# Score banks in a ring of five and a single y bank, in an attention kernel with two fused layers

## The reference

```
x = x + 0.5 * ffn(layernorm(x))
x = x + attn(layernorm(x))
x = x + 0.5 * ffn(layernorm(x))

ffn(x)  = x @ W.T + b + (x @ V_r) @ C.T          # 256 -> 256, rank 32 correction
attn(x): 16 heads of 16; causal; no softmax:
    att = polymax(q @ k.T / sqrt(16))
    y   = att @ v;   return y @ W_proj
polymax(s) = (s**2 + 1) / 1000        for s > 0
             (1 - s / 100) / 1000     for -100 <= s <= 0
             0                        below -100, and where masked
```

## Time and profile before

| | |
|---|---|
| median of 3 runs | 2130.39 us (2128.72 to 2139.16) |
| the profiled execution | 2134.19 us, span 2132.5 us |
| TensorE (PE) busy | 1797.4 us, 84% |
| VectorE (DVE) busy | 1707.9 us, 80% |
| ScalarE (ACT) busy | 1261.1 us, 59% |
| GpSimd (POOL) busy | 511.1 us, 24% |
| granted TensorE clock | 0.965 of full speed |
| DMA | 181.02 MB, 85 GB/s |

### The profile page before, as it was taken

One profiled execution on the slowest core, in us unless ns is written; L12 is line 12 of the kernel. 1 busy time (PEld: TensorE's weight loads), 2 busy tenths in 40 slices (PEclk: granted clock), 3 DMA queues, 4 the chain that ended last, 5 costly groups with the idle time before them and its releaser, 6 DMA issues.

```text
span 2132.5 us, 33455 instructions
## 1 busy us (share of the span) xinstructions
PE 1797.4 (84%) x12694; PEld 762.1 (36%) x12694; DVE 1707.9 (80%) x2609; ACT 1261.1 (59%) x1090; POOL 511.1 (24%) x746
## 2 busy tenths in 40 slices
PE   4777888898989888898988889898888888888885
PEld 3544333232334333343433334343332222223333
DVE  2466788888888888888888888888888989898882
ACT  1244467666666666666666666666666666666561
POOL 3232223131312224122222412232231111110121
PEclk9898899999999999999999999999999999999997
DMA  2343331313223241322414133332313221213111
GB/s 78 121 127 108 116 123 57 97 58 99 81 85 112 61 127 59 94 81 85 121 59 120 54 101 90 85 113 67 117 57 92 60 74 56 75 56 87 55 33 53
DMA packets 155049, 181.02 MB, mean 85 GB/s; under 512 B 22012, under 2 KB 129660, under 8 KB 152836
## 3 DMA queue, kind: packets, MB, share of 16 engines
q1 hardware_dynamic: 154884, 178.82, 28.3%
HBM read 102.43 MB, written 76.30 MB: 84 GB/s over the span
## 4 chain that ended last, share of the span: by engine, by line
PE 49%; DVE 35%; issue 9%; ACT 4%; DMA 2%; POOL 1%; SPq 0%; DVEq 0%; ACTq 0%; POOLq 0%
DVE rp L826 24%; PE y_ps L891 19%; PE bank L891 14%; PE score L891 13%; DVE lin L832 4%; DVE bnst_ln L851 2%; ACT rp L755 2%; PE bank L910 2%; DVE qk_max L838 1%; POOL z L640 1%; DMA part_scratch<-parts 1%; DVE rest L410 1%; DMA out_dram<-x 1%; DVE st_add L813 0%; DVE parts L412 0%
## 5 line engine op out<-in xcount | busy, mean ns | idle before, releaser
L826 DVE TENSOR_SCALAR rp<-score 128x1024 f32<-128x1024 f32 (+3 forms) x1280 | 1318.7, 1056 | 174.4 <-PE score L891 169.4
L755 ACT ACTIVATE rp<-rp 128x2048 f32<-128x2048 f32 (+3 forms) x640 | 1056.7, 1653 | 640.7 <-DVE rp L826 426.3
L891 PE MATMUL score<-qs,ks 96*128 96x512 bf16 (+3 forms) x2560 | 686.5, 354 | 246.9 <-DVE rp L826 126.7
L891 PE MATMUL y_ps<-rp,vt 128*16 128x512 f32 (+3 forms) x5120 | 605.0, 545 | 0.0
L661 POOL TENSOR_SCALAR_AFFINE_SELECT rp<-rp 128x512 f32<-128x512 f32 x256 | 162.3, 634 | 1224.8 <-DVE rp L826 1222.6
L891 PEld LDWEIGHTS score<-qs,ks 96*128 96x128 bf16 x2560 | 197.1, 98 | 658.4 <-DVE rp L826 498.6
L832 DVE SCALAR_TENSOR_TENSOR lin<-score,slope_mask 128x256 f32<-128x256 f32 x512 | 212.0, 414 | 0.0
L891 PE MATMUL bank<-w_ffn,zT 128*128 128x256 f32 x512 | 170.3, 431 | 4.5 <-ACT zT L718 4.5
L891 PE MATMUL bank<-w_qkv,z2T 128*128 128x256 f32 x512 | 157.8, 409 | 8.9 <-ACT parts L734 8.9
L891 PEld LDWEIGHTS y_ps<-rp,vt 128*16 128x16 f32 x5120 | 84.2, 95 | 222.8 <-issue 169.3
L891 PEld LDWEIGHTS bank<-w_ffn,zT 128*128 128x128 f32 x512 | 95.8, 207 | 98.9 <-issue 64.1
(11 more groups left out here) (72 smaller groups left out, 986.3 us busy)
## 6 DMA issues: line engine op xcount, KB each, us to landing
part_scratch<-parts SPq DMA_DIRECT2D x16, 1536.0 KB, 5.8
qs<-part_scratch SPq DMA_DIRECT2D x384, 64.0 KB
ks<-part_scratch SPq DMA_DIRECT2D x384, 64.0 KB, 2.3
state_scratch<-st_new SPq DMA_DIRECT2D x16, 528.0 KB
st<-state_scratch SPq DMA_DIRECT2D x64, 132.0 KB
x_sb<-in_L_attn_x_dram SPq DMA_DIRECT2D x16, 512.0 KB, 4.3
x_scratch<-x SPq DMA_DIRECT2D x16, 512.0 KB, 5.2
qT_scratch<-qkT SPq DMA_DIRECT2D x16, 512.0 KB, 3.5
```

What stands on the lines that cost most here:

```text
L755: nc.scalar.activation(buf, buf, ACT.Square, scale=SCALE).then_inc(squared, 1)
L826: nc.vector.tensor_scalar(rp[T % RP_BUFS][:, 2 * u:2 * u + 2, off:CH], score[H % S_BUFS][:, :, off:CH], 0.0, RISE / SCALE, ALU.max, ALU.ad ...
L891: return nc.tensor.matmul(*args, start=start, stop=stop, skip_group_check=True)
```

## The change

The eight PSUM banks are handed out anew. The four score banks and one of the two y banks make one ring of five banks, `score`; y has a single bank.

Half H writes banks 2H mod 5 and (2H+1) mod 5. The wait for half H-2 now stands before the second of its two matmuls, and the first has no wait of its own (`banks_of`, `head_of`). VectorE still reads a half in one instruction where its banks are neighbours. Where H mod 5 is 2, they are banks 4 and 0, and both the raise and the lin become two instructions, one a bank (`runs_of`). A window's first product now waits for the copy of the window before (`y_copied`, w) and not of the one before that. The setup uses two score banks where it had used the y banks. The corrections for very low scores behind the main part (`lows`), which these inputs do not call for, are renamed to match.

```diff
-S_BUFS, RP_BUFS, L_BUFS = 2, 5, 5
+S_BANKS, RP_BUFS, L_BUFS = 5, 5, 5
...
-        score = [ps(f"score{i}", [P, 2, CH]) for i in range(S_BUFS)]
-        y_ps = [ps(f"y_ps{i}", [P, CH]) for i in range(2)]
+        score = ps("score", [P, S_BANKS, CH])
+        y_ps = ps("y_ps", [P, CH])
         bank = [ps(f"bank{i}", [P, CH]) for i in range(2)]
...
+        def banks_of(H):
+
+            return 2 * H % S_BANKS, (2 * H + 1) % S_BANKS
+
+        def runs_of(H):
+
+            first, second = banks_of(H)
+            u = 2 * (H % 2)
+            if second:
+                return [(score[:, first:second + 1, :], slice(u, u + 2))]
+            return [(score[:, 0:1, :], slice(u, u + 1)), (score[:, first:first + 1, :], slice(u + 1, u + 2))]
+
+        def head_of(H, bank_number):
+            return 2 * (H % 2) + int(bank_number == max(banks_of(H)))
...
-                nc.scalar.activation(y_sb[w % 2][:], y_ps[w % 2][:], ACT.Copy).then_inc(y_copied, 1)
+                nc.scalar.activation(y_sb[w % 2][:], y_ps[:], ACT.Copy).then_inc(y_copied, 1)
...
-                    nc.vector.tensor_scalar(rp[T % RP_BUFS][:, 2 * u:2 * u + 2, off:CH], score[H % S_BUFS][:, :, off:CH],
-                                            0.0, RISE / SCALE, ALU.max, ALU.add).then_inc(raised, 1)
+                    for src, heads in runs_of(H):
+                        ins = nc.vector.tensor_scalar(rp[T % RP_BUFS][:, heads, off:CH], src[:, :, off:CH],
+                                                      0.0, RISE / SCALE, ALU.max, ALU.add)
+                    ins.then_inc(raised, 1)
...
+                        for src, heads in runs_of(H):
+                            ins = nc.vector.scalar_tensor_tensor(lin[D % L_BUFS][:, heads, :], src[:, :, off:off + P],
+                                                                 ONE / (SLOPE * SCALE), slope_mask[:, 0:heads.stop - heads.start, :],
+                                                                 ALU.add, ALU.mult)
+                        ins.then_inc(lin_done, 1)
...
-                if H >= S_BUFS:
-                    pe.wait_ge(raised, H - S_BUFS + 1)
-                    if is_diag((H - S_BUFS) // 2):
-                        pe.wait_ge(lin_done, diag_halves(H - S_BUFS))
-                for v in range(2):
-                    head = 2 * u + v
-                    ins = mm(score[H % S_BUFS][:, v, off:CH], ks[:, head, P * kb:P * kb + P],
+
+                for bank_number in banks_of(H):
+                    if bank_number == banks_of(H)[1] and H >= 2:
+                        pe.wait_ge(raised, H - 1)
+                        if is_diag((H - 2) // 2):
+                            pe.wait_ge(lin_done, diag_halves(H - 2))
+                    head = head_of(H, bank_number)
+                    ins = mm(score[:, bank_number, off:CH], ks[:, head, P * kb:P * kb + P],
                              qs[:, head, CH * c + off:CH * c + CH])
...
-                y = y_ps[w % 2]
+                y = y_ps
                 if t == FIRST[c]:
-                    if w >= 2:
-                        pe.wait_ge(y_copied, w - 1)
+                    if w >= 1:
+                        pe.wait_ge(y_copied, w)
```

More of the change, by code:

```diff
@@ L704, in _ @@
             act.wait_ge(setup_pe, 1)
-            nc.scalar.activation(vrT[:], score[0][0:32, 0, 0:DM], ACT.Copy).then_inc(setup_act, 1)
-            nc.scalar.activation(cT[:], score[0][0:32, 0, DM:2 * DM], ACT.Copy).then_inc(setup_act, 1)
+            nc.scalar.activation(vrT[:], score[0:32, 0, 0:DM], ACT.Copy).then_inc(setup_act, 1)
+            nc.scalar.activation(cT[:], score[0:32, 0, DM:2 * DM], ACT.Copy).then_inc(setup_act, 1)
             for k in range(KC):
                 act.wait_ge(setup_pe, 2 + k)
-                nc.scalar.activation(w_ffn[:, k, :], y_ps[k][:, 0:DM], ACT.Copy, scale=0.5).then_inc(setup_act, 1)
+                nc.scalar.activation(w_ffn[:, k, :], score[:, 1 + k, 0:DM], ACT.Copy, scale=0.5).then_inc(setup_act, 1)
             act.wait_ge(const_ready, CONSTS)
@@ L831, in slot @@
                             dve.wait_ge(pv_done, diag_tile(D - L_BUFS) + 1)
-                        nc.vector.scalar_tensor_tensor(lin[D % L_BUFS][:, 2 * u:2 * u + 2, :], score[H % S_BUFS][:, :, off:off + P],
-                                                       ONE / (SLOPE * SCALE), slope_mask[:, 0:2, :], ALU.add, ALU.mult).then_inc(lin_done, 1)
+                        for src, heads in runs_of(H):
[3 more added lines that the diff above has]
+                        ins.then_inc(lin_done, 1)
                 for x in o.empties.get(s - 1, ()):
@@ L873, in correct @@
                     c, kb, off = TILES[h // 2]
-                    sc = score[0][:, :, off:CH]
+                    sc = score[:, 0:2, off:CH]
                     line = rp[0][:, 0:2, off:CH]
@@ L883, in correct @@
                         dve.wait_ge(low_y_loaded, (n * CPB + (c + 1)) * (16 * QH))
-                        nc.vector.tensor_tensor(y_sb[1][:], y_ps[0][:], y_sb[0][:], ALU.add).then_inc(low_added, 1)
+                        nc.vector.tensor_tensor(y_sb[1][:], y_ps[:], y_sb[0][:], ALU.add).then_inc(low_added, 1)
             lows(dve, correct, slot)
@@ L895, in _ @@
             for k in range(KC):
-                nc.tensor.transpose(score[0][0:32, 0, P * k:P * k + P], vr_in[:, k, :], ident[:])
-                ins = nc.tensor.transpose(score[0][0:32, 0, DM + P * k:DM + P * k + P], c_in[:, k, :], ident[:])
+                nc.tensor.transpose(score[0:32, 0, P * k:P * k + P], vr_in[:, k, :], ident[:])
+                ins = nc.tensor.transpose(score[0:32, 0, DM + P * k:DM + P * k + P], c_in[:, k, :], ident[:])
             ins.then_inc(setup_pe, 1)
@@ L901, in _ @@
                 for j in range(KC):
-                    dst = y_ps[k][:, P * j:P * j + P]
+                    dst = score[:, 1 + k, P * j:P * j + P]
                     mm(dst, w_in[:, j, P * k:P * k + P], ident[:], start=True, stop=False)
@@ L1014, in correct @@
                     c, kb, off = TILES[h // 2]
-                    y = y_ps[0]
+                    y = y_ps
                     if h == 2 * FIRST[c]:
@@ L1021, in correct @@
                         head = 2 * (h % 2) + v
-                        ins = mm(score[0][:, v, off:CH], ks[:, head, P * kb:P * kb + P], qs[:, head, CH * c + off:CH * c + CH])
+                        ins = mm(score[:, v, off:CH], ks[:, head, P * kb:P * kb + P], qs[:, head, CH * c + off:CH * c + CH])
                     ins.then_inc(low_scored, 1)
```

## The result

The changed kernel took 2252.7 us (median of 4 runs, 2247.5 to 2257.3), the kernel before 2133.4 us beside it. The ratio is 1.0557, with a 95% interval of 1.0519 to 1.0596: 5.6% slower, about 119 us. I had said 2.4% and a range that ended at 2225 us. The direction was right and the size was not.

The account below looks back on a forecast made before the run. Neither TensorE (84% busy) nor VectorE (80%) was full; work going back and forth between them set the end. Copy wait +63, score lead -22 and splits +9 made +50 us: 2181 us, 2.4% slower, 8-in-10 range 2150 to 2225.

Parts of the forecast that it names:

- Part 1: At 60 window starts on TensorE, the first product waits for ScalarE's copy of the window before: +63 us.
- the clock: Rival, on TensorE: new idle lowers the granted clock to a mean of 0.92, adding 51 us, 2232 us; chance 8%.
- absorbed-wait rival: At window starts, the score matmuls' lead hides the copy wait, so it costs nothing: 2102 us; chance 5%.
- the sum: Whole kernel: copy wait, score lead and split reads together, 63 - 22 + 9 = +50 us.
- Part 2: At 114 VectorE-to-TensorE handovers, one score matmul instead of two follows the raise: -22 us; 59 at window starts bring nothing.
- Part 3: On VectorE, 336 added instructions from split reads, 0.062 us each with 43% on the path: +9 us.
- full-price rival: On VectorE, the splits cost their full duration everywhere, 50 us, for +91 us in all, 2221 us; chance 10%.
- a granted clock under 0.95: Sign on TensorE that the prediction is wrong; it expected the clock to stay near 0.96.

## Why the prediction was wrong, point by point

**Part 1, the wait of one y bank: right.** Sixty starts wait, the handover behind the copy is 0.05 us (1028.29 + 0.58 = 1028.87 to 1028.92 or 1028.93), little or nothing of it is absorbed, and the cost without the clock is 57 us (51 to 62) where 63 were said. The absorbed-wait rival was wrong for the reason given.

**The step that failed** is the clock. In the sum it had no term; it stood only as a rival, at 8% and 51 us, with the argument that "the new idle comes in pieces of 1 us, between stretches of dense work". That argument was never read from a row. Pieces of this length did lower it here: the single y bank lost 64 us to the clock and the change 75. I had guessed the mean well (0.92, and 0.926 came), but weighed the rival as unlikely, and drew the range to 2225 us, under its own 2232. The rival's price was low too. It spread the loss over the 49% of the chain that is TensorE's; at 0.926 that gives 1045 x (0.965 / 0.926 - 1) = 44 us, and 75 came. As an estimate from the two levels of the clock (full or half), its mean puts 333 us of the changed kernel at half speed and 149 of the kernel before. The 184 us more cost TensorE half their length, 92 us, near the 99 us by which it is busier, and 75 of 92 is 82% on the path. Of the 333 us 191 lie in the 7 us behind the window starts, where TensorE is the late engine, and of the 149 only 18, so nearly all that came on top lies there. The trace of before held a warning, in TensorE's timeline some 20 us ahead of the earlier trace rows:

```profile
962.31 0.59 PE L891 MATMUL score<-qs,ks 96*128 96x512 bf16 x2 [1.65 <-DVE lin L832]
...
965.20 1.04 PE L891 MATMUL score<-qs,ks 96*128 96x512 bf16 x2 [0.46 <-DVE rp L826]
966.16 1.91 PE L891 MATMUL y_ps<-rp,vt 128*16 128x512 f32 x8
```

Behind idle pieces of 1.65 and 0.46 us a pair of scores takes 1.04 us and not 0.59, and the values 1.91 and not 1.05: half speed, in the middle of the dense part, and the granted clock reads 0.50 from 964 to 970 us. Also the waits don't come alone. At the start of window 27 the changed kernel idles 0.33, 0.59 and 0.84 us for raise, raise and copy within 2.5 us, so the new wait joins two gaps that were there before. The kernel before has them at the same place, 0.46 and 0.61 us, and its clock stays at 1.00 behind them.

The clock record of this case's traces holds only 0.5 and 1.0 of full speed, and 0.54 is the mean of the 7 us behind the start of window 27. In the 5 us ahead of that start TensorE was idle for no more than 0.84 us at a time.

**Part 2, the ring's lead: the mechanism right, the size at most somewhat low.** I said 22 us for 114 handovers and left out the 59 at window starts. In the changed kernel it is 57 + 17 - 43 = 31 us, if the terms add, and the three intervals leave some 10 us either way, so that 22 isn't ruled out. With the copy first, where all 173 handovers count, my figure is 173 x 0.215 x 0.9 = 33 us, and the runs give 29 to 40, by what the splits cost in the ring. The timeline of the changed kernel shows it as foretold:

```profile
1053.01 2.42 DVE L843 TENSOR_SCALAR rp<-score 128x1024 f32<-128x1024 f32 x3
...
1053.39 0.38 PE L912 MATMUL score<-qs,ks 96*128 96x512 bf16 x1
...
1054.30 0.39 PE L912 MATMUL score<-qs,ks 96*128 96x512 bf16 x1 [0.52 <-DVE rp L843]
```

The first matmul of a pair runs 0.9 us before the second, while VectorE still reads. At full clock one score matmul alone takes 0.38 us and a pair 0.59 to 0.61, so by estimate 0.15 to 0.17 us of a pair behind a wait is a delay that doesn't grow with the second matmul. The prediction had 0.60 - 0.43 = 0.17.

**Part 3, the splits: the price right, the share low**, 17 us for 9. The full-price rival (50 us) is out. By the middle values the errors of parts 2 and 3 go against each other, 9 us less and 8 us more.

So the sum without the clock was 50 and came to 43; the 75 us are one missing term. The prediction had named a granted clock under 0.95 as a sign of being wrong, and that is the sign that came.

## What to carry to other kernels

Where a change puts new waits of even 1 us on a nearly full TensorE (84% busy here), price them twice: once as the wait, and once as what the engine may do behind it at half speed. Here the second was the larger part, 75 of 119 us. If the wait can't be avoided, matmuls into an unused bank before it can help: here they gave 64 to 75 us back, and no cost of their own showed (57 us left for the wait, 63 worked out). Better is to look at what stands before the awaited instruction in its own engine's list. The second y bank only covered for a copy that stood behind a square; with the copy first one bank was enough, and the freed bank was worth 23 us as part of the scores' ring.

## What the runs showed of the hardware that was not expected

- Idle pieces of 0.3 to 1.3 us of TensorE before 60 starts brought the mean granted clock from 0.965 to 0.935 (single y bank) and 0.926 (the change). As the clock is either full or half in the traces, a mean of 0.926 over 2252 us is 333 us of halved clock, against 149 us before.
- Whether a start lost its clock went with the length of the idle piece, but not by a sharp limit: in the change 42 of the 45 starts with 0.8 us or more did, and 2 of the 19 with less; with the single y bank alone 25 of 29, and 15 of 35.
- Behind a start the halving could take in nearly the whole next stretch of work: 2.08 and 1.91 us for products of 1.06 and 1.05.
- 408 matmul instructions of pure filling made the single-bank kernel of 12694 faster by 3%, and the same ones behind the wait made it some 0.6% slower, 15 us (13 either way) for 53 us of products.
